# Feed forward of a decoder layer: outputs split by tiles of tokens, gate units in threes, two banks for the last down projections

## The chip, the cores and the metric

The kernel is one program on one core of a Trainium2 chip. The number is the device time of an execution in microseconds. In the profile PE is TensorE, DVE VectorE, ACT ScalarE, POOL GpSimd and SP the engine that only issues transfers.

## What is computed

A decoder layer in float32, with a layer norm behind each part. Cut to what matters:

```python
x = layernorm(x + self_attention(x))                     # x: 32 x 100 x 512, 3200 tokens
x = layernorm(x + cross_attention(x, ctx_1024))          # 16 heads of 32, context 32 x 722 x 512
gate = x @ (w_gate / 127).T                              # w_gate, w_up: 1536 x 512 integers
up = x @ (w_up / 127).T
x = layernorm(x + (silu(gate) * up) @ (w_down / 127).T)  # w_down: 512 x 1536
```

The change touches what happens from the output projection of the cross attention on.

## The kernel before

The program runs in stages: self attention; cross attention; and a last one, which this document calls the feed forward. It takes the 3200 tokens in `NG` = 5 groups of `GT` = 640, a group in `TT` = 5 tiles of 128 tokens or in two halves of 320. To keep float32 accuracy, an activation is split into a high part (rounded to the format of the fast products, written by ScalarE) and a low part (what is left, by VectorE or GpSimd), and TensorE sums the products of both.

The order of each engine's instructions is written out by hand; semaphores hold the engines together, and the names of the semaphores say what has been done. For a group `g` the work is:

- `gate_and_up(g)` on TensorE: `HU` = 24 units, one for each chunk of 128 hidden features and each half of the group; 8 products of 320 columns into `ps_g` and 8 into `ps_u`, with two banks each. `silu_and_high` (ScalarE), `gate` (VectorE) and `low_h` (GpSimd) turn a unit into the high and low half of the hidden activations `hs`. The function `unit(u)` says which chunk and half the unit `u` is.
- `down(g, i)` for each tile `i` on TensorE: 24 products of 512 columns into the single bank `ps_d`. VectorE takes it with `third_sum` (adds `x2`, then statistics), GpSimd computes the factor (`rstd_of`), and VectorE norms with `third_norm`; the tile is stored.
- between those, for the group ahead, `project_o(g+1, i)`: 12 products of 512 columns from the split outputs of the cross attention, `acts`, into the single bank `ps_y`; `second_sum` and `normalise("a", ...)` on VectorE make the tile `x2`; `transpose_x2(g+1, i-1)` transposes it with four products into `ps_t`, and `high_x2` (ScalarE) and `low_x2` (VectorE) split it into `acts` again, now the input of the next gate units.

The body of the loop on TensorE shows this order:

```python
gate_and_up(g)
for i in range(TT):
    down(g, i)
    project_o(g + 1, i)
    if i:
        transpose_x2(g + 1, i - 1)
```

The last tile's transpose, `transpose_x2(g, TT - 1)`, stands behind the first gate unit of its group. `acts` can be overwritten with the next group's outputs only when the last gate unit has read them; then `high_o` (ScalarE) and `low_o` (VectorE) split the raw tile `oraw`, before in `KD` = 4 chunks of 128 features by 640 tokens. On VectorE `low_o(g+1)` stands ahead of `third_sum(g, 0)`. Group 0 and the last group are written apart; in group 0 the weights are still arriving and ScalarE converts them between the units (`CONVERT_AT`), and the last two `weighted_sum` of the cross attention are done there (`RESULT_AT`). In the last group only the five `down` are left behind the units.

## Time and profile before

| what | us |
|---|---|
| median of 3 runs | 2518.63 |
| lowest and highest | 2517.06, 2522.48 |
| the profiled execution | 2520.11 |
| its span, first to last instruction | 2518.3 |
| TensorE busy in the span | 2437.4 |

The span is what the trace covers; the profiled execution's own time is 1.8 us longer. A row of the order of time gives an instruction's start, its duration, its engine and line, what it writes and reads, and in brackets how long the engine stood idle before it and who released it.

### The profile page before, as it was taken

How to read it: one execution, taken by the hardware profiler on the slowest of the kernel's cores; microseconds unless marked ns; L12 is line 12 of the kernel's file. 1: busy time of each engine (PE TensorE's matmuls, PEld its weight loads, DVE VectorE, ACT ScalarE, POOL GpSimd, SP SyncE). 2: the span in 40 equal slices, each digit the busy share in tenths (PEclk: the TensorE clock that was granted, in tenths of full speed). 3: DMA queues.
4: the chain of work that ended last, by engine and by line, in shares of the span. 5: the costliest groups of instructions: out<-in, count | busy, mean ns of one | idle time of the engine just before them, and what ended most of it. 6: DMA issues, size and time to landing. Idle time of an engine off the chain costs nothing.

```text
span 2518.3 us, 58619 instructions
## 1 busy us (share of the span) xinstructions
PE 2437.4 (97%) x22240; PEld 2089.1 (83%) x22240; DVE 1532.8 (61%) x2589; ACT 1253.1 (50%) x2451; POOL 1323.4 (53%) x1058
## 2 busy tenths in 40 slices
PE   7999998988999999999999999999999899999998
PEld 7888866887888888888888888888888698998997
DVE  7555567863666666666667666666666725335342
ACT  3544453104666666666666666666666651221311
POOL 4766554314656666665666666565665532333332
PEclk9999988998999999999999999999999999999999
DMA  7554455633777766777777777777777841101010
GB/s 226 164 149 140 131 155 200 243 125 106 191 189 193 189 186 183 188 189 187 194 190 189 185 183 190 188 187 193 189 188 191 233 137 63 39 25 63 0 38 22
DMA packets 259625, 391.61 MB, mean 156 GB/s; under 512 B 123164, under 2 KB 140572, under 8 KB 259356
## 3 DMA queue, kind: packets, MB, share of 16 engines
q1 hardware_dynamic: 234780, 337.66, 46.8%
q10 hardware_dynamic: 24576, 50.36, 8.3%
q8 instruction: 169, 2.77, 0.5%
q14 instruction: 100, 0.82, 0.1%
HBM read 134.11 MB, written 52.43 MB: 74 GB/s over the span
## 4 chain that ended last, share of the span: by engine, by line
PE 63%; issue 8%; DVE 2%; DMA 1%; SPq 1%; POOL 1%; ACT 1%; POOLq 0%; ACTq 0%; DVEq 0%
PE D_ps_p L68 41%; PE D_ps_s L1719 7%; PE D_ps_p L1745 6%; PE E_ps_g L68 3%; PE E_ps_u L68 3%; PE E_ps_d L68 2%; PE E_ps_y L68 1%; SPq L1171 1%; DMA D_pT<-D_turned 1%; POOL E_hidden_low L1322 0%; DVE D_neg_max L1529 0%; DMA E_w_int<-in_w_gate 0%; POOL E_rstd_a L1309 0%; DVE D_turned L1543 0%; ACT D_e L1394 0%
## 5 line engine op out<-in xcount | busy, mean ns | idle before, releaser
L1278 POOL TENSOR_SCALAR D_e<-D_e,D_inv 128x722 f32<-128x722 f32 x256 | 538.9, 2105 | 539.3 <-DVE D_inv L1535 539.3
L1394 ACT ACTIVATE D_e<-D_ps_s,D_neg_max 128x723 f32<-128x723 f32 x512 | 438.2, 862 | 409.4 <-DVE D_neg_max L1529 358.7
L1529 DVE TENSOR_REDUCE D_neg_max<-D_ps_s 128x1 f32<-128x723 f32 x512 | 439.5, 899 | 313.4 <-PE D_ps_s L1719 313.4
L1543 DVE STREAM_TRANSPOSE D_turned<-D_e 128x768 f32<-128x768 f32 x512 | 496.2, 972 | 6.6 <-DMA D_pT<-D_turned 6.1
L68 PE MATMUL D_ps_p<-D_ctx_high,cross_wk_high 128*128 128x362 f32 (+1 forms) x1024 | 351.1, 343 | 12.4 <-DVE D_ctx_low L1560 12.3
L68 PE MATMUL D_ps_p<-D_ctx_low,cross_wk_high 128*128 128x362 f32 (+1 forms) x1024 | 337.4, 329 | 0.0
L68 PE MATMUL D_ps_p<-D_ctx_high,cross_wk_low 128*128 128x362 f32 (+1 forms) x1024 | 335.9, 328 | 0.0
L68 PE MATMUL D_ps_p<-cross_wv_high,D_ctx_high 128*128 128x512 f32 (+1 forms) x768 | 303.8, 396 | 0.0
L68 PE MATMUL D_ps_p<-cross_wv_high,D_ctx_low 128*128 128x512 f32 (+1 forms) x768 | 303.3, 395 | 0.0
L68 PE MATMUL D_ps_p<-cross_wv_low,D_ctx_high 128*128 128x512 f32 (+1 forms) x768 | 301.7, 393 | 0.0
L1401 ACT ACTIVATE D_e<-D_e,D_inv 128x722 f32<-128x722 f32 x256 | 231.0, 902 | 8.0 <-DVE D_inv L1535 8.0
L68 PEld LDWEIGHTS D_ps_p<-D_ctx_high,cross_wk_high 128*128 128x128 f32 x1024 | 193.3, 189 | 35.1 <-issue 32.1
L1293 POOL TENSOR_TENSOR D_ctx_low<-D_craw,D_ctx_high 128x722 fp32r<-128x722 f32 x124 | 198.9, 1604 | 17.4 <-issue 6.8
L1322 POOL TENSOR_TENSOR E_hidden_low<-E_gated,E_hidden_high 128x320 fp32r<-128x320 f32 x120 | 105.2, 878 | 189.0 <-ACT E_hidden_high L1459 189.0
L68 PEld LDWEIGHTS D_ps_p<-D_ctx_low,cross_wk_high 128*128 128x128 f32 x1024 | 194.1, 190 | 2.7
L1719 PE MATMUL D_ps_s<-D_keys,D_queries 32*128 32x241 f32 (+1 forms) x3072 | 193.5, 380 | 2.7 <-ACT D_e L1394 2.7
L68 PEld LDWEIGHTS D_ps_p<-D_ctx_high,cross_wk_low 128*128 128x128 f32 x1024 | 193.9, 189 | 0.0
L1639 DVE SCALAR_TENSOR_TENSOR E_gated<-E_ps_u,E_gated 128x320 f32<-128x320 f32 x120 | 58.9, 491 | 215.5 <-ACT E_gated L1466 215.5
L1719 PEld LDWEIGHTS D_ps_s<-D_keys,D_queries 32*128 32x128 f32 x3072 | 135.1, 185 | 60.9 <-issue 50.6
L68 PEld LDWEIGHTS D_ps_p<-cross_wv_high,D_ctx_low 128*128 128x128 f32 (+1 forms) x768 | 139.1, 181 | 39.6
L1389 ACT ACTIVATE D_values<-D_ps_p 128x512 f32<-128x512 f32 x192 | 114.4, 596 | 106.4 <-PE D_ps_p L68 105.9
L68 PEld LDWEIGHTS D_ps_p<-cross_wv_low,D_ctx_high 128*128 128x128 f32 (+1 forms) x768 | 139.7, 182 | 29.7
(189 smaller groups left out, 5087.5 us busy)
## 6 DMA issues: line engine op xcount, KB each, us to landing
D_pT<-D_turned SPq DMA_DIRECT2D x1536, 96.0 KB, 2.8
D_pT<-D_turned ACTq DMA_DIRECT2D x512, 96.0 KB, 2.9
D_craw<-in_ctxT SPq DMA_DIRECT2D x126, 361.0 KB, 3.8
self_q<-A_q_out SPq DMA_DIRECT2D x10, 640.0 KB, 3.8
self_k<-A_k_out SPq DMA_DIRECT2D x10, 640.0 KB, 3.2
self_v<-A_v_out SPq DMA_DIRECT2D x25, 256.0 KB, 2.1
A_q<-self_q SPq DMA_DIRECT2D x32, 200.0 KB, 3.9
A_k<-self_k SPq DMA_DIRECT2D x32, 200.0 KB, 4.3
```

Source lines behind the costliest of these rows:

```text
L68: last = pe.matmul(out, lhs(a, k), rhs(b, k), start=(k == 0 and n == 0), stop=(k == chunks - 1 and n == len(terms) - 1))
L1278: pool.tensor_scalar(head, head, inv[:, 2 * (s % 2):2 * (s % 2) + 1], None, ALU.mult)\
L1293: pool.tensor_tensor(cs[b % 2][1][:, k, :], craw[k % 2][:, :], cs[b % 2][0][:, k, :].bitcast(F32), ALU.subtract).then_inc(c_low, 1)
L1322: pool.tensor_tensor(hs[1][:, c, cols], gated[u % 2][:, :], hs[0][:, c, cols].bitcast(F32), ALU.subtract).then_inc(hl_done, 1)
L1389: act.activation(vs[b % 2][0:rows, i, :], bank("v", b, i)[0:rows, 0:D], ACT.Copy).then_inc(v_done, 1)
L1394: act.activation(e[n // 2 % 2][:, n % 2, 0:PARTS * PART].rearrange("p (a c) -> p a c", a=PARTS), parts_of(n), ACT.Exp, bias=neg_max[:, n % ...
L1401: act.activation(head, head, ACT.Copy, scale=inv[:, 2 * (s % 2) + 1:2 * (s % 2) + 2])\
L1529: dve.tensor_reduce(neg_max[:, n % 4:n % 4 + 1], parts_of(n), AX.XY, ALU.max, negate=True)\
L1543: dve.transpose(turned[quad % 2][:, :, 2 * (s % 2) + h, :].rearrange("p j (t r) -> p t j r", r=32), e[s % 2][:, h, :].rearrange("p (t j r) ...
L1639: dve.scalar_tensor_tensor(gated[u % 2][:, :], ps_u[u % 2][:, 0:HALF], FSCALE, gated[u % 2][:, :], ALU.mult, ALU.mult).then_inc(h_done, 1)
L1719: return pe.matmul(of_head[:, j, a, 0:end - first], qs[rows, m, :, :].rearrange("p a q -> p (a q)"), ks[rows, m, first:end], start=True, s ...
L1745: last = pe.matmul(out[HD * j:HD * (j + 1), 0:T], vs[b % 2][:, i, c:c + HD], pT[quad % 2][:, :, j, 32 * i:32 * i + QB], start=(i == 0), st ...
```

## The change

Four things change. The outputs of the cross attention are split in five operations of 4 x 128 elements, one for each tile of tokens, instead of four of 640, and each `project_o` waits only for its own tile. The gate units go in threes: three chunks for the first half of the group, then the same three for the second half (before in pairs); the first unit that reads the second half is now `u == 3`. The last tile is transposed, and its high and low halves made, behind the second unit instead of the first. In the last group the down projections use `ps_d` and `ps_y` in turn, and wait for the sum of the tile two before.

```diff
--- before.py
+++ after.py
@@ -1111,7 +1111,7 @@
 
 
 
-            return 2 * (u // 4) + u % 2, u // 2 % 2
+            return 3 * (u // 6) + u % 3, u // 3 % 2
 
         def groups(eng, body):
 
@@ -1129,6 +1129,10 @@
                 return (w_gate, w_up)[n % 2].rearrange("(k p) n -> p k n", p=P)[:, :, n // 2 * FC:(n // 2 + 1) * FC]
             k = (n - 2 * KD) * (KF // KD)
             return w_down[k * P:(k + KF // KD) * P, :].rearrange("(a p) n -> p a n", p=P)
+
+        def split_before(g):
+
+            return KD + TT * (g - 1) if isinstance(g, int) else g * TT + (KD - TT)
 
         def x1_rows(g, i):
 
@@ -1175,7 +1179,7 @@
 
                 def load_o(g):
                     if later(g):
-                        sp.wait_ge(o_low, KD * g)
+                        sp.wait_ge(o_low, split_before(g))
                     sp.dma_start(oraw[:, :, :], eo_rows[:, :, col(g * GT, GT)]).then_inc(o_loaded, 16)
 
                 def load_x1(g, i):
@@ -1437,8 +1441,9 @@
                     act.wait_ge(o_loaded, 16 * g + 16)
                     if later(g):
                         act.wait_ge(gu_done, HU * g)
-                    for k in range(KD):
-                        act.activation(acts[0][:, k, :], oraw[:, k, :], ACT.Copy).then_inc(o_high, 1)
+                    for i in range(TT):
+                        cols = slice(i * P, (i + 1) * P)
+                        act.activation(acts[0][:, :, cols], oraw[:, :, cols], ACT.Copy).then_inc(o_high, 1)
 
                 def high_x2(g, i):
                     act.wait_ge(t_done, TT * g + i + 1)
@@ -1465,10 +1470,10 @@
                         wait(act, hl_done, n - 1)
                         act.activation(gated[u % 2][:, :], ps_g[u % 2][:, 0:HALF], ACT.Silu, scale=FSCALE)\
                            .then_inc(silu_done, 1)
-                        if u == 0:
+                        if u > 0:
+                            high(u - 1)
+                        if u == 1:
                             high_x2(g, TT - 1)
-                        else:
-                            high(u - 1)
                         if not later(g):
                             for piece_n in CONVERT_AT.get(u, ()):
                                 convert(piece_n)
@@ -1605,21 +1610,22 @@
                     dve.wait_ge(x1b_done, n + 1)
                     add_and_stats("a", n, lambda dst: dve.tensor_tensor(dst, ps_y[:, :], x1_rows(g, i), ALU.add))
 
-                def third_sum(g, i):
+                def third_sum(g, i, down=ps_d):
                     n = TT * g + i
                     dve.wait_ge(d_done, n + 1)
                     add_and_stats("b", n, lambda dst: dve.scalar_tensor_tensor(
-                        dst, ps_d[:, :], FSCALE, x2[:, i, :], ALU.mult, ALU.add))
+                        dst, down[:, :], FSCALE, x2[:, i, :], ALU.mult, ALU.add))
 
                 def third_norm(g, i):
                     wait(dve, out_stored[i % 2], 16 * slot_count(g, i))
                     normalise("b", TT * g + i, y[i % 2][:, :])
 
                 def low_o(g):
-                    for k in range(KD):
-                        dve.wait_ge(o_high, KD * g + k + 1)
+                    for i in range(TT):
+                        cols = slice(i * P, (i + 1) * P)
+                        dve.wait_ge(o_high, split_before(g) + i + 1)
                         dve.wait_ge(o_loaded, 16 * g + 16)
-                        dve.tensor_tensor(acts[1][:, k, :], oraw[:, k, :], acts[0][:, k, :].bitcast(F32),
+                        dve.tensor_tensor(acts[1][:, :, cols], oraw[:, :, cols], acts[0][:, :, cols].bitcast(F32),
                                           ALU.subtract).then_inc(o_low, 1)
 
                 def low_x2(g, i):
@@ -1638,7 +1644,7 @@
                         dve.wait_ge(silu_done, n + 1)
                         dve.scalar_tensor_tensor(gated[u % 2][:, :], ps_u[u % 2][:, 0:HALF], FSCALE, gated[u % 2][:, :],
                                                  ALU.mult, ALU.mult).then_inc(h_done, 1)
-                        if u == 0:
+                        if u == 1:
                             low_x2(g, TT - 1)
                         if not later(g) and u in RESULT_AT:
                             take_result(RESULT_AT[u])
@@ -1686,7 +1692,7 @@
                 groups(dve, body)
                 gate(NG - 1)
                 for i in range(TT):
-                    third_sum(NG - 1, i)
+                    third_sum(NG - 1, i, (ps_d, ps_y)[i % 2])
                     third_norm(NG - 1, i)
 
             @block.tensor
@@ -1752,9 +1758,10 @@
 
                 def project_o(g, i):
                     n = TT * g + i
-                    if i == 0:
-                        pe.wait_ge(o_low, KD * (g + 1))
-                    if not later(n):
+                    if later(g):
+                        pe.wait_ge(o_low, split_before(g) + i + 1)
+                    elif i == 0:
+                        pe.wait_ge(o_low, KD)
                         pe.wait_ge(wo_low, KD)
                         pe.wait_ge(k_done, KU * B)
                         pe.wait_ge(v_done, ST * B)
@@ -1784,7 +1791,7 @@
                                 pe.wait_ge(int_done, 2 * (c // 3 + 1))
                             if u == 0:
                                 pe.wait_ge(tl_done, TT * g + (HALF + P - 1) // P)
-                            if u == 2:
+                            if u == 3:
                                 pe.wait_ge(tl_done, TT * (g + 1))
                             wait(pe, h_done, n - 1)
                             for ps, which in ((ps_g, 0), (ps_u, 1)):
@@ -1792,22 +1799,24 @@
                                                 lambda a, k: place(w, 2 * (c // 3) + which)[:, k, c % 3 * P:(c % 3 + 1) * P],
                                                 lambda a, k: view(acts[a][:, k, h * HALF:(h + 1) * HALF]))
                             last.then_inc(gu_done, 1)
-                            if u == 0:
+                            if u == 1:
                                 transpose_x2(g, TT - 1)
                             if not later(g) and u in RESULT_AT:
                                 weighted_sum(RESULT_AT[u])
 
-                    def down(g, i):
+                    def down(g, i, out=ps_d):
                         n = TT * g + i
                         if not later(g) and i == 0:
                             pe.wait_ge(int_done, PIECES)
                             pe.wait_ge(o_done, QUADS * B)
                         if i == 0:
-                            pe.wait_ge(hl_done, HU * (g + 1) - 2)
+                            pe.wait_ge(hl_done, HU * (g + 1) - 3)
                         if i == 2:
                             pe.wait_ge(hl_done, HU * (g + 1))
-                        wait(pe, sum_done["b"], n)
-                        products(pe, ps_d[:, :], ((0, 0), (1, 0)), KF,
+                        if out is ps_y:
+                            pe.wait_ge(sum_done["a"], TT * NG)
+                        wait(pe, sum_done["b"], n - (1 if isinstance(g, int) and g == NG - 1 and i else 0))
+                        products(pe, out[:, :], ((0, 0), (1, 0)), KF,
                                  lambda a, k: view(hs[a][:, k, i * P:(i + 1) * P]),
                                  lambda a, k: w[2 * KD + k // 3][:, k % 3 * D:(k % 3 + 1) * D]).then_inc(d_done, 1)
 
@@ -1830,7 +1839,7 @@
                     groups(pe, body)
                     gate_and_up(NG - 1)
                     for i in range(TT):
-                        down(NG - 1, i)
+                        down(NG - 1, i, (ps_d, ps_y)[i % 2])
 
                 for s in range(FIRST, MAIN + 1):
                     if 0 <= s < STEPS and s % 2 == 0:
```

ScalarE at the start of a group in the loop: the silu and the hidden copy of units 0 and 1 (`E_gated`, `E_hidden_high`), and the last tile's high half from `E_ps_t0`. Before:

```order
L1466 ACTIVATE E_gated0_8136<-E_ps_g0 128x320 [waits E_hl_done]
L1444 ISA
L1445 ACTIVATE E_acts_high_8112<-E_ps_t0 128x4x128 [waits E_t_done]
L1464 REGISTER_ALU
L1466 ACTIVATE E_gated1_8137<-E_ps_g1 128x320 [waits E_hl_done,E_gu_done]
L1459 ACTIVATE E_hidden_high_8138<-E_gated0_8136 128x320 [waits E_h_done]
L1464 REGISTER_ALU
L1466 ACTIVATE E_gated0_8136<-E_ps_g0 128x320 [waits E_hl_done,E_gu_done]
```

and now:

```order
L1471 ACTIVATE E_gated0_8136<-E_ps_g0 128x320 [waits E_hl_done]
L1469 REGISTER_ALU
L1471 ACTIVATE E_gated1_8137<-E_ps_g1 128x320 [waits E_hl_done,E_gu_done]
L1464 ACTIVATE E_hidden_high_8138<-E_gated0_8136 128x320 [waits E_h_done]
L1449 ISA
L1450 ACTIVATE E_acts_high_8112<-E_ps_t0 128x4x128 [waits E_t_done]
L1469 REGISTER_ALU
L1471 ACTIVATE E_gated0_8136<-E_ps_g0 128x320 [waits E_hl_done,E_gu_done]
L1464 ACTIVATE E_hidden_high_8138<-E_gated1_8137 128x320 [waits E_h_done]
```

The high half of the last tile has moved from behind the first silu to behind the second silu and the first hidden copy.

VectorE at the boundary behind group 0: `low_o(1)` from `E_oraw`, then the sum and the statistics of the first down projection (`E_ps_d`). Before:

```order
L1639 SCALAR_TENSOR_TENSOR E_gated_8137<-E_ps_u,E_gated_8137 128x320 [waits E_silu_done,E_gu_done]
L1622 TENSOR_TENSOR E_acts_low<-E_oraw,E_acts_high 128x640 [waits E_o_loaded,E_o_high] x4
L1611 SCALAR_TENSOR_TENSOR E_r_b<-E_ps_d,E_x_8134 128x512 [waits E_d_done]
L1590 BN_STATS E_stats_b<-E_r_b 128x6 [waits E_sum_b]
L1592 BN_AGGR E_mv_b<-E_stats_b 128x2 [waits E_stat_b]
L1594 TENSOR_SCALAR E_var_eps_b<-E_mv_b 128x1 [waits E_mv_b]
```

and now:

```order
L1645 SCALAR_TENSOR_TENSOR E_gated_8137<-E_ps_u,E_gated_8137 128x320 [waits E_silu_done,E_gu_done]
L1628 TENSOR_TENSOR E_acts_low<-E_oraw,E_acts_high 128x4x128 [waits E_o_loaded,E_o_high] x5
L1616 SCALAR_TENSOR_TENSOR E_r_b<-E_ps_d,E_x_8134 128x512 [waits E_d_done]
L1595 BN_STATS E_stats_b<-E_r_b 128x6 [waits E_sum_b]
L1597 BN_AGGR E_mv_b<-E_stats_b 128x2 [waits E_stat_b]
L1599 TENSOR_SCALAR E_var_eps_b<-E_mv_b 128x1 [waits E_mv_b]
```

Four operations on 640 elements have become five on 4 x 128, all of them still ahead of the sum.

TensorE in the last group, from the end of the first down projection to the start of the second (the weights are `E_w_f32r8` to `11`). Before:

```order
L68 MATMUL E_ps_d<-E_w_f32r11_8175,E_hidden_low_8139 128x512
L68 MATMUL E_ps_d<-E_w_f32r11_8175,E_hidden_high_8138 128x512
L68 MATMUL E_ps_d<-E_w_f32r11_8175,E_hidden_low_8139 128x512
L68 MATMUL E_ps_d<-E_w_f32r8_8172,E_hidden_high_8138 128x512 [waits E_sum_b]
L68 MATMUL E_ps_d<-E_w_f32r8_8172,E_hidden_low_8139 128x512
L68 MATMUL E_ps_d<-E_w_f32r8_8172,E_hidden_high_8138 128x512
```

and now:

```order
L68 MATMUL E_ps_d<-E_w_f32r11_8175,E_hidden_low_8139 128x512
L68 MATMUL E_ps_d<-E_w_f32r11_8175,E_hidden_high_8138 128x512
L68 MATMUL E_ps_d<-E_w_f32r11_8175,E_hidden_low_8139 128x512
L68 MATMUL E_ps_y<-E_w_f32r8_8172,E_hidden_high_8138 128x512 [waits E_sum_b,E_sum_a]
L68 MATMUL E_ps_y<-E_w_f32r8_8172,E_hidden_low_8139 128x512
L68 MATMUL E_ps_y<-E_w_f32r8_8172,E_hidden_high_8138 128x512
```

The second projection writes to another bank and waits for sums that lie further back.

## Rows read from the trace of the kernel before

**Rows 1.** The page, busy time, share of the span and instructions.
```profile
PE 2437.4 (97%) x22240; PEld 2089.1 (83%) x22240; DVE 1532.8 (61%) x2589; ACT 1253.1 (50%) x2451; POOL 1323.4 (53%) x1058
```

**Rows 2.** The waits of TensorE from 2005 us on: total, times, longest.
```profile
PE E_ps_y L68 <- DVE E_acts_low L1622: 4.8, 4, 1.2
...
PE E_ps_d L68 <- DVE E_r_b L1611: 3.2, 4, 0.9
PE E_ps_t L1771 <- DVE E_x L1599: 2.5, 5, 0.7
PE E_ps_g L68 <- DVE E_gated L1639: 1.7, 1, 1.7
```

**Rows 3.** TensorE in order of time at a group's boundary: start, duration.
```profile
2180.89 0.39 PE L68 MATMUL E_ps_d<-E_w_f32r,E_hidden_low 128*128 128x512 f32 x1
...
2182.49 0.50 PE L68 MATMUL E_ps_y<-E_wo_high,E_acts_high 128*128 128x512 f32 x1 [1.21 <-DVE E_acts_low L1622]
...
2185.13 0.39 PE L68 MATMUL E_ps_y<-E_wo_high,E_acts_low 128*128 128x512 f32 x1
2185.36 0.39 PE L68 MATMUL E_ps_d<-E_w_f32r,E_hidden_high 128*128 128x512 f32 x1
...
2190.57 0.39 PE L68 MATMUL E_ps_d<-E_w_f32r,E_hidden_low 128*128 128x512 f32 x1
...
2193.29 0.40 PE L68 MATMUL E_ps_y<-E_wo_high,E_acts_low 128*128 128x512 f32 x1
...
2193.89 0.48 PE L68 MATMUL E_ps_d<-E_w_f32r,E_hidden_high 128*128 128x512 f32 x1
```

**Rows 4.** The other engines at that boundary; last, the subtractions' minimum, median, maximum (ns).
```profile
2178.14 4.29 DVE L1622 TENSOR_TENSOR E_acts_low<-E_oraw,E_acts_high 128x640 fp32r<-128x640 f32 x4 [1.26 <-ACT E_acts_high L1441]
2182.35 0.68 DVE L1611 SCALAR_TENSOR_TENSOR E_r_b<-E_ps_d,E_x 128x512 f32<-128x512 f32 x1
2177.29 2.61 ACT L1441 ACTIVATE E_acts_high<-E_oraw 128x640 fp32r<-128x640 f32 x4
2178.40 1.88 POOL L1304 TENSOR_TENSOR E_x1b<-E_x1b,E_bo_b 128x512 f32<-128x512 f32 x1
L1622 DVE TENSOR_TENSOR E_acts_low<-E_oraw,E_acts_high x4: 810/894/1917, 2178.1 to 2181.6; 128x640 fp32r<-128x640 f32 x4
```

**Rows 5.** A group's start: TensorE, ScalarE, VectorE; L1459 by line.
```profile
2222.12 0.31 PE L68 MATMUL E_ps_u<-E_acts_low,E_w_f32r 128*128 128x320 f32 x1
2222.90 0.66 PE L1771 MATMUL E_ps_t<-ident,E_x 128*128 128x128 f32 x4 [0.47 <-DVE E_x L1599]
2223.31 0.39 PE L68 MATMUL E_ps_g<-E_acts_high,E_w_f32r 128*128 128x320 f32 x1
...
2225.74 0.31 PE L68 MATMUL E_ps_g<-E_acts_high,E_w_f32r 128*128 128x320 f32 x1
2222.55 0.44 ACT L1466 ACTIVATE E_gated<-E_ps_g 128x320 f32<-128x320 f32 x1 [1.82 <-PE E_ps_u L68]
2223.59 0.60 ACT L1445 ACTIVATE E_acts_high<-E_ps_t 128x512 fp32r<-128x512 f32 x1 [0.61 <-PE E_ps_t L1771]
L1459 ACT ACTIVATE E_hidden_high<-E_gated 128x320 fp32r<-128x320 f32 x120 | 55.6, 463 | 1.4 <-DVE E_gated L1639 1.4
2224.29 0.69 DVE L1629 TENSOR_TENSOR E_acts_low<-E_ps_t,E_acts_high 128x512 fp32r<-128x512 f32 x1 [0.45 <-ACT E_acts_high L1445]
```

**Rows 6.** Group 0 in order of time: TensorE's transposes, ScalarE's third conversion.
```profile
2014.56 0.66 PE L1771 MATMUL E_ps_t<-ident,E_x 128*128 128x128 f32 x4 [0.39 <-DVE E_x L1599]
2025.11 1.49 ACT L1497 ACTIVATE E_w_f32r<-E_w_int 128x1536 fp32r<-128x1536 int32 x1 [2.98 <-DMA E_w_int<-in_w_gate]
```

**Rows 7.** First and last product of the last group's five down projections.
```profile
2480.80 0.39 PE L68 MATMUL E_ps_d<-E_w_f32r,E_hidden_high 128*128 128x512 f32 x1
2512.23 0.39 PE L68 MATMUL E_ps_d<-E_w_f32r,E_hidden_low 128*128 128x512 f32 x1
```

**Rows 8.** The last 38 us: busy times by engine, then the granted clock (0.98).
```profile
2480.00:2518.30 38.30, 29.39 (x127) 22.82 (x125) 11.83 (x26) 1.27 (x3) 4.87 (x8) 0.98 0.10 36
```

## The prediction

> **What bounds the kernel now.** I read the page first, then the waits of the last stage, then that stage in order of time. The page has TensorE busy for 97% of the span [rows 1]; the other engines reach at most 61%. The change touches the feed forward alone, the last 507 us, so its worth is read there: whatever it takes from another engine is worth nothing unless TensorE stood still for it. The list of waits from 2005 us on names the idle times of TensorE [rows 2]: 4.8 us in four waits of `project_o`, the cross attention's output projection, for the low halves of its activations; 3.2 us in four waits of a down projection for the sum that empties its bank; 2.5 us in five waits of the transposes for the normalised tile; 1.7 us once for a gated product. The change aims at all but the last. An idle time is less than what a stall costs, since the first product after it starts slowly, so I take each cost as a difference between first and last starts in order of time.
>
> **The change, part by part.** Four parts; each is costed on TensorE.
>
> *The split of the cross attention's outputs by tiles of tokens.* Before, `project_o(g+1, 0)` waits until all four chunks are split. From the start of the last product of the down projection before it to the start of its own last product 4.24 us pass (2180.89 to 2185.13); where nothing is missing it is 2.72 us (2190.57 to 2193.29) [rows 3]. The stall costs 1.52 us, and there are four such places [rows 2]: 6.1 us. Afterwards tile 0 needs one ScalarE and one VectorE operation. ScalarE starts the copies at 2177.29 and VectorE the first subtraction at 2178.14; four take 4.29 us, one of them 1.92 us and the shortest 0.81 [rows 4]. Even if the long one comes first, tile 0 is split by 2178.1 + 1.9 = 2180.0, and TensorE asks for it at 2180.89 + 0.23 = 2181.12. So the whole 1.52 us goes. What is late next is `third_sum(g, 0)`: it stands behind all of `low_o` on VectorE, and `down(g, 1)` waits for it, since both use `ps_d`. It began at 2182.35 and took 0.68 [rows 4]; with as many elements in five operations instead of four I put it at the same place plus 0.1, done by 2183.15. TensorE will want the bank at 2181.12 + 2.72 = 2183.84. The cover is 0.7 us, and before it was 2.3 us (2185.36). Nothing else on VectorE or GpSimd is pushed: the second sum and both norms follow the earlier projection.
>
> The price of an operation on 4 x 128 elements from the raw tile is not in the trace. From below it is the 0.69 us of the subtraction of 4 x 128 from PSUM [rows 5], from above the 1.92 us of the slowest subtraction of 640 [rows 4]. I take 0.7 for those undisturbed and one delay of 1.1 us as before (1.92 less 0.81), which gives 0.7 x 5 + 1.1 = 4.6, less small overlaps. The long row lies beside GpSimd's addition at 2178.40, which took 1.88 us [rows 4]; only GpSimd's last subtraction and that one addition are queued there, so five small operations meet the same two instructions.
>
> The Trainium skill says (VectorE: DVE Perf Modes, on the TRN2 errata) that each instruction from SBUF pays a fixed cost, and gives (N+151)/0.96 ns for such a subtraction. The trace agrees at 640: 824 ns against the fastest, 810. By it five of 512 cost 0.16 us more than four of 640, which would speak against the split but stays inside its cover. It also says (SBUF — State Buffer, Who interferes with whom) that a VectorE operation with two SBUF inputs and a GpSimd operation that reads SBUF shut each other out for a whole instruction; the 1.92 and 1.88 us side by side agree, and by that rule there is again one delay, not five.
>
> *The last tile's transposes, behind the second gate unit instead of the first.* Before, TensorE ended the first unit at 2222.12 (start of its last product) and could transpose only at 2222.90, and the next unit began at 2223.31: 1.19 us [rows 5]. Where the tile is there, last product to first product across a transpose is 0.60 us (2193.29 to 2193.89) [rows 3]. The loss is 0.59 for an idle time of 0.47, thus 0.12 above it. The five waits hold 2.5 us, 0.39 of them in group 0 [rows 2, 6]; the other four cost 2.1 + 4 x 0.12 = 2.6 us. The tile's norm ends about when it did, and one more unit (2.43 us, 2223.31 to 2225.74) lies ahead of the transpose, so this wait goes entirely.
>
> It is replaced by a tighter one. The low half of the tile must be there at the fourth unit (`u == 3`) instead of the third. Counted from the start of the second unit's last product: ScalarE starts the silu 0.43 later (2222.12 to 2222.55) and needs 0.44, then the copy of the hidden half, 0.46, then the tile's high half, 0.60; VectorE starts 0.70 after that last one starts and needs 0.69 [rows 5]. That is 0.43 + 0.44 + 0.46 + 0.70 + 0.69 = 2.72. TensorE comes to the fourth unit at 0.60 + 2.43 = 3.03. There are 0.3 us left, where before 2225.74 less 2224.98 left 0.8. I cost it at nothing.
>
> *Units in threes.* 24 units a group of the same 16 products each; only the order of chunk and half changes. `down(g, 0)` now waits for 21 of 24 low halves instead of 22, all of the first half of the group, so it asks for less. Nothing.
>
> In group 0 there is a wait that stays. ScalarE's third conversion there stood still for 2.98 us for a transfer of weights and began at 2025.11 [rows 6]; the silu behind it was late, and TensorE stood still for 1.7 us [rows 2]. That transfer hangs on nothing in the change, and the conversion keeps its place at `u == 2`. Whatever TensorE gains before (the 0.39 us) it waits longer here. I count nothing in group 0 up to the end of that wait.
>
> *Two banks in the last group.* The five down projections run from 2480.80 to 2512.23 (first start to last start), 31.43 us [rows 7]. Unhindered, one is 5.21 us from first to last start (2185.36 to 2190.57) and 0.23 to the next [rows 3]: 4 x 5.44 + 5.21 = 26.97. That saves 4.5 us. Each sum and norm ends well within the 5.44 us of the next projection, and with `sum_done` asked for two tiles back no wait is left. What follows 2512.23, 6.1 us to the end of the span, stays.
>
> **Sum.** 6.1 + 2.6 + 4.5 = 13.2 us. The profiled execution took 2520.1 us (span 2518.3 and 1.8 around it), so it would become 2506.9. It lies 1.5 us above the median of the runs, 2518.63, and against that the sum gives 2505.5 us, my forecast. TensorE's granted clock reads 0.98 in the stretch with the pauses of the last five projections, close to the full 2.4 GHz [rows 8], so fewer pauses change no product's rate by more than that.
>
> **Rivals.**
> 1. *The boundary's gain is given back one projection later*: `third_sum(g, 0)` is late and `down(g, 1)` waits. For it speaks that the cover is just 0.7 us and that `low_o` was once held up by 1.1 us. Against it, that one hold-up is already in my time. If it took two delays more, 0.7 us would be covered and 1.5 of 2.2 lost at each of four places: all 6.1 us, and the time is 2511.6. Chance 12%.
> 2. *The fourth unit waits for the last tile's low half.* ScalarE's queue is the reason: one more copy ahead of it, 0.3 us of cover. If each link takes 0.25 us more than in the rows, 0.7 us are lost in four groups, 2.8 us: 2508.3. Chance 8%.
> 3. *The change does little at the starts and ends of groups*: both stalls are formed anew in full, and only the two banks count: 2514.1. It needs 1 and 2 together at full size. Chance 5%.
> 4. *Slower.* The strided operations of `low_o` all cost the upper bound: 2178.1 + 5 x 1.92 = 2187.7, the sum ends at 2188.4, and `down(g, 1)` starts 3.0 us later than the 2185.36 of before, which is 12.0 us in four groups against 2.6 + 4.5 gained elsewhere: 2523.5. It decides from 1.75 us a group, so when the five take 8.4 us or 1.7 each. For it there is the one of four at that price [rows 4], against it that the GpSimd work beside them ends after two instructions. Chance 3%.
> 5. *More than the sum*: the transfer in group 0 lands early enough, or the first tiles gain too; at most 0.4 + 1.7 more, 2503.4. Chance 4%.
>
> **Numbers.** My forecast has 68%. The three runs lie from 1.6 us below their median to 3.9 above; its own range is 2503 to 2508.5. Rivals 1 and 2 reach to 2511.6, rival 5 with a fast run to 2501.9. From 2501.5 to 2512 about 2 in 10 or less is left out (rivals 3 and 4, and the spread of the runs). A change under 0.2% (5.0 us) can't be told from none: rival 3 and a part of 4 and of 1 fall there, 8%; slower 3%; faster 89%.
>
> **What would show it.** In the profile after: no wait of `E_ps_y` for `E_acts_low` and none of `E_ps_d` for `E_r_b` in the last group; no wait of the transposes for `E_x` except in group 0; groups 2.1 us closer together; five down projections in 27.0 us. A new wait of `E_ps_d` for `E_r_b` behind the first projection of a group shows rival 1 and, from 3 us on, rival 4; one of `E_ps_g` for `E_acts_low` shows rival 2. The prediction is wrong if the five subtractions take over 5.3 us together.

## The result

The changed kernel takes 2507.75 us (median of 5 runs, 2503.35 to 2510.46) against 2518.63 before; the ratio is 0.9949, with 0.9933 to 0.9964 as its interval. Measured again, beside two of the kernels below, it was 0.9959 (0.9946 to 0.9973), 2507.80 us. The forecast was 2505.5, range 2501.5 to 2512. The profiled execution took 2508.33 us, its span 2506.5: 11.8 us less than the span of before, where the sum had 13.2.

The page's busy line, to compare with [rows 1]: TensorE does the same products in 11.8 us less span, and its share is still 97%.

```profile
PE 2432.2 (97%) x22240; PEld 2089.1 (83%) x22240; DVE 1535.0 (61%) x2593; ACT 1251.4 (50%) x2455; POOL 1319.6 (53%) x1058
```

The waits of TensorE from 2005 us on, in the changed kernel (total, times, longest), to compare with [rows 2]:

```profile
PE E_ps_y L68 <- DVE E_r_a L1611: 3.2, 1, 3.2
PE E_ps_g L68 <- DVE E_gated L1645: 2.7, 1, 2.7
PE E_ps_g L68 <- DVE E_acts_low L1635: 1.1, 1, 1.1
```

The four waits of `project_o` for the low halves, the four of the last down projections for the sum and all five of the transposes are gone. The wait of 3.2 us is the one that was there before, ahead of group 0. The wait for a gated product has grown from 1.7 to 2.7 us.

**A group's boundary.** TensorE in order of time: the last product of the first down projection, the first and last of `project_o`, and the next down projection.

```profile
2180.16 0.39 PE L68 MATMUL E_ps_d<-E_w_f32r,E_hidden_low 128*128 128x512 f32 x1
...
2180.38 0.39 PE L68 MATMUL E_ps_y<-E_wo_high,E_acts_high 128*128 128x512 f32 x1
...
2182.88 0.39 PE L68 MATMUL E_ps_y<-E_wo_high,E_acts_low 128*128 128x512 f32 x1
2183.10 0.39 PE L68 MATMUL E_ps_d<-E_w_f32r,E_hidden_high 128*128 128x512 f32 x1
...
2188.32 0.39 PE L68 MATMUL E_ps_d<-E_w_f32r,E_hidden_low 128*128 128x512 f32 x1
```

From 2180.16 to 2182.88 are 2.72 us, where [rows 3] had 4.24. VectorE beside it, and the five subtractions by tile (minimum, median, maximum in ns):

```profile
2177.31 4.46 DVE L1628 TENSOR_TENSOR E_acts_low<-E_oraw,E_acts_high 128x512 fp32r<-128x512 f32 x5 [1.16 <-ACT E_acts_high L1446]
2181.69 0.68 DVE L1616 SCALAR_TENSOR_TENSOR E_r_b<-E_ps_d,E_x 128x512 f32<-128x512 f32 x1
```

```profile
L1628 DVE TENSOR_TENSOR E_acts_low<-E_oraw,E_acts_high x5: 678/679/1780, 2177.3 to 2181.1; 128x512 fp32r<-128x512 f32 x5
```

Five operations on 4 x 128 elements take 4.46 us, four of 640 took 4.29 [rows 4]. Three of the five take 0.68 us; the first takes 0.95, and the second again takes long, 1.78, beside GpSimd's addition. Before, it was the same two: 0.98 and 1.92 us, the others 0.81. The sum ends at 2182.37 and TensorE asks for the bank at 2183.10: a cover (time to spare before TensorE would have to wait) of 0.7 us, as forecast.

**A group's start.** TensorE with the last tile's transposes, now behind the second unit, and VectorE's low half of that tile:

```profile
2222.21 0.31 PE L68 MATMUL E_ps_u<-E_acts_low,E_w_f32r 128*128 128x320 f32 x1
2222.36 0.60 PE L1778 MATMUL E_ps_t<-ident,E_x 128*128 128x128 f32 x4
2222.72 0.39 PE L68 MATMUL E_ps_g<-E_acts_high,E_w_f32r 128*128 128x320 f32 x1
...
2225.15 0.31 PE L68 MATMUL E_ps_g<-E_acts_high,E_w_f32r 128*128 128x320 f32 x1
2223.95 0.69 DVE L1635 TENSOR_TENSOR E_acts_low<-E_ps_t,E_acts_high 128x512 fp32r<-128x512 f32 x1 [0.36 <-ACT E_acts_high L1450]
```

From the last product before the transposes to the first behind them are 0.51 us, against 1.19 in [rows 5]. The low half is done at 2224.64; the unit that needs it starts at 2225.15. So 0.5 us are left; I had forecast 0.3.

**The last group.** First product of the first, first product of the second (into the other bank), and last product of the fifth down projection:

```profile
2473.44 0.39 PE L68 MATMUL E_ps_d<-E_w_f32r,E_hidden_high 128*128 128x512 f32 x1
...
2478.90 0.39 PE L68 MATMUL E_ps_y<-E_w_f32r,E_hidden_high 128*128 128x512 f32 x1
...
2500.44 0.39 PE L68 MATMUL E_ps_d<-E_w_f32r,E_hidden_low 128*128 128x512 f32 x1
```

These are 27.00 us from first to last, where [rows 7] had 31.43; 26.97 was forecast.

**Group 0.** TensorE before and behind its pause, and ScalarE's third conversion:

```profile
2024.87 0.31 PE L68 MATMUL E_ps_u<-E_acts_low,E_w_f32r 128*128 128x320 f32 x1
2027.89 0.39 PE L68 MATMUL E_ps_g<-E_acts_high,E_w_f32r 128*128 128x320 f32 x1 [2.70 <-DVE E_gated L1645]
...
2028.40 0.31 PE L68 MATMUL E_ps_g<-E_acts_low,E_w_f32r 128*128 128x320 f32 x1
...
2029.50 0.47 PE L68 MATMUL E_ps_u<-E_acts_high,E_w_f32r 128*128 128x320 f32 x1
...
2031.77 1.37 PE L1751 MATMUL D_ps_p<-D_pT,D_values 128*32 128x100 f32 x48
2025.34 1.48 ACT L1502 ACTIVATE E_w_f32r<-E_w_int 128x1536 fp32r<-128x1536 int32 x1 [4.01 <-DMA E_w_int<-in_w_gate]
```

The conversion behind the transfer of weights starts almost when it did (2025.34 against 2025.11 in [rows 6]), but TensorE comes earlier and stands still for 2.70 us, 1.03 more than before. Counted from the first gate product of group 0 (2011.40, before 2011.58), TensorE begins its last product ahead of the pause at 13.47 us, before at 14.10: that is 0.6 of the 1.03 us. The conversion begins at 13.94, before at 13.53: the other 0.4 is a later transfer. Then something new: the products of 320 columns, 0.31 us long at 2028.40, are 0.47 us long at 2029.50. The stages show why (the number behind the busy times is the granted clock):

```profile
2024.00:2028.00 4.00, 1.30 (x10) 1.06 (x9) 0.49 (x1) 2.17 (x3) 0.42 (x1) 1.00 0.04 15
2028.00:2030.00 2.00, 2.00 (x10) 2.00 (x11) 0.49 (x1) 0.79 (x2) 1.04 (x2) 0.67 0.00 0
2030.00:2032.00 2.00, 2.00 (x15) 1.67 (x18) 0.00 (x0) 0.13 (x1) 0.27 (x1) 0.50 0.00 0
2032.00:2034.00 2.00, 2.00 (x54) 1.85 (x47) 0.77 (x2) 0.67 (x2) 0.87 (x1) 0.98 0.04 12
```

The clock reads 0.50, the lower level of 1.2 GHz, from 2030 to 2032; in all it is low for 3.4 us, which this document calls a slow stretch. Before, behind the pause of 1.67 us, it was full:

```profile
2026.00:2028.00 2.00, 0.34 (x2) 0.37 (x3) 0.49 (x1) 1.27 (x3) 0.65 (x1) 1.00 0.00 0
2028.00:2030.00 2.00, 2.00 (x16) 1.98 (x14) 0.49 (x1) 0.80 (x2) 1.03 (x2) 1.00 0.00 0
```

From the pause's end to the weighted sum (2027.89 to 2031.77) pass 3.88 us; before it was 2.51 for the same work (2027.66 to 2030.17). The slow stretch alone costs 1.4 us.

### The profile page after: what moved, and what is told of

It reads as the page before. It is cut to its first block, busy times and chain, and to the rows that moved or that the text cites. A ratio compares the mean times of both kernels' runs of the same rounds, so it can differ in the third digit from the quotient of the medians.

```text
span 2506.5 us, 58637 instructions
## 1 busy us (share of the span) xinstructions
PE 2432.2 (97%) x22240; PEld 2089.1 (83%) x22240; DVE 1535.0 (61%) x2593; ACT 1251.4 (50%) x2455; POOL 1319.6 (53%) x1058
## 4 chain that ended last, share of the span: by engine, by line
PE 72%; DVE 1%; issue 1%; DMA 1%; SPq 1%; ACT 1%; POOL 0%; ACTq 0%; DVEq 0%; POOLq 0%
PE D_ps_p L68 41%; PE D_ps_s L1725 7%; PE D_ps_p L1751 6%; PE E_ps_u L68 5%; PE E_ps_g L68 5%; PE E_ps_d L68 5%; PE E_ps_y L68 3%; SPq L1175 1%; ACT D_e L1398 0%; DVE D_neg_max L1534 0%; PE E_ps_t L1778 0%; DMA D_pT<-D_turned 0%; DMA E_w_int<-in_w_gate 0%; DVE D_turned L1548 0%; DMA D_values<-in_ctxT 0%
```

## The experiments

Each ratio is to the kernel before as measured on the same chip. The runs of one kernel lie 3 to 12 us apart, and what lies ahead of the first gate product makes much of that: in the twelve profiled executions of this study it starts between 2009.40 and 2014.19 us. Two times of a few us apart are therefore read in three pieces of one trace each, from a start to a start of TensorE's products, which leave that out: group 0 (first gate product to first down projection), the groups between (to the first down projection of the last group) and the last five projections (to their last product).

| kernel | ratio to before (interval) | group 0 | between | last five | pause in group 0 |
|---|---|---|---|---|---|
| before | | 62.12 | 407.10 | 31.43 | 1.67 |
| changed | 0.9949 (0.9933 to 0.9964) | 64.01 | 398.03 | 27.00 | 2.70 |
| changed, again | 0.9959 (0.9946 to 0.9973) | 62.08 | 398.03 | 27.00 | 2.26 |
| split alone | 0.9966 (0.9953 to 0.9979) | 60.87 | 400.96 | 31.45 | 0.42 |
| threes and late transposes alone | 0.9985 (0.9976 to 0.9994) | 64.52 | 404.11 | 31.44 | 3.18 |
| two banks alone | 0.9987 (0.9977 to 0.9997) | 62.18 | 406.99 | 26.99 | 1.72 |
| changed, late conversion | 0.9933 (0.9921 to 0.9946) | 59.58 | 398.03 | 26.99 | none |
| the same, again | 0.9933 (0.9919 to 0.9946) | 59.58 | 398.02 | 27.00 | none |
| before, late conversion | 0.9989 (0.9980 to 0.9998) | 60.23 | 406.94 | 31.48 | none |
| late transposes in pairs | 1.0036 (1.0022 to 1.0050) | 62.23 | 413.79 | 31.44 | 1.60 |
| subtractions twice | 1.0006 (0.9996 to 1.0016) | 62.76 | 409.91 | 27.00 | 2.91 |
| before, early conversion | 1.0018 (1.0008 to 1.0028) | 66.85 | 407.00 | 31.44 | 4.86 |

The pieces "between" and "last five" repeat within 0.2 us where the kernels do the same there. Group 0 does not, for the transfer of weights comes at another time in each execution: the third conversion begins 13.53 us behind the first gate product before, 13.58 with two banks alone, 12.27 with the split alone, 14.42 with the threes and late transposes alone, 13.94 and 13.49 in the two traces of the changed kernel, 14.17 with the subtractions twice. TensorE's last product ahead of the pause begins at 14.09 or 14.10 in the kernels whose order of units and transposes is the old one and at 13.47 to 13.50 where it is the new one. In all nine traces with a pause, those of the early conversion (14.37 and 11.75) and of the late transposes in pairs (13.63 and 14.28) included, the pause is the first of these numbers less the second plus 2.24 us, to 0.01. So 0.6 us of a pause come from the change, and the rest of its differences from the transfer.

**The split alone.** The kernel before with `high_o`, `low_o`, `split_before` and the waits of `project_o` and of the load from the changed one:

```diff
-                    for k in range(KD):
-                        act.activation(acts[0][:, k, :], oraw[:, k, :], ACT.Copy).then_inc(o_high, 1)
+                    for i in range(TT):
+                        cols = slice(i * P, (i + 1) * P)
+                        act.activation(acts[0][:, :, cols], oraw[:, :, cols], ACT.Copy).then_inc(o_high, 1)
```

> The kernel before with only the split of the cross attention's outputs by tiles. Theory of additive stalls: the four waits of TensorE for E_acts_low vanish, 4 x 1.52 = 6.1 us less, 2512.5 us; the wait in group 0 stays near 1.7 us and the clock full there, since nothing ahead of it is earlier. Rival (given back one projection later): a wait of the second down projection for E_r_b at each of four boundaries, and a time above 2515.

Measured: 2513.41 us, 8.0 below the 2521.46 of before on that chip. The groups between are 6.14 us shorter, as the theory had it, and no wait of a down projection for `E_r_b` came up between them. That group 0 keeps its pause of 1.7 us did not come true: it was 1.25 us shorter in this execution and its pause 0.42 us, since the transfer came 1.26 us earlier (12.27 against 13.53). The part does not touch it.

**The units in threes and the late transposes alone.** `unit`, the places of `transpose_x2`, `high_x2` and `low_x2` and the two counts:

```diff
-            return 2 * (u // 4) + u % 2, u // 2 % 2
+            return 3 * (u // 6) + u % 3, u // 3 % 2
...
-                            if u == 0:
+                            if u == 1:
                                 transpose_x2(g, TT - 1)
```

> The kernel before with only the units in threes and the last tile's transposes behind the second unit. Theory that group 0 gives a part back because of this part: four group starts gain 3.0 us, TensorE comes earlier to the wait for the converted weights in group 0, stands still for over 2 us instead of 1.7, and then runs for some 4 us at the lower clock, 1.4 to 1.7 us lost; 2517 us. Rival (the longer pause and the lower clock were chance in that run and have nothing to do with the change): 3.0 us gained whole, 2515.6 us, clock full behind the pause.

Measured: 2517.46 us. Between the groups 2.99 us less. In group 0 the pause is 3.18 us, and behind it the way to the weighted sum takes 3.43 us instead of 2.51 at the slow clock:

```profile
2029.39 0.39 PE L68 MATMUL E_ps_g<-E_acts_high,E_w_f32r 128*128 128x320 f32 x1 [3.18 <-DVE E_gated L1639]
...
2032.82 1.50 PE L1745 MATMUL D_ps_p<-D_pT,D_values 128*32 128x100 f32 x30
2026.84 1.48 ACT L1497 ACTIVATE E_w_f32r<-E_w_int 128x1536 fp32r<-128x1536 int32 x1 [4.49 <-DMA E_w_int<-in_w_gate]
```

So group 0 is 2.4 us longer and the part is worth 0.6 us net in this trace. That is what the theory had, but not all of it is due to the part: of the 1.51 us by which the pause is longer, 0.9 come from a late transfer (the last row, 14.42 us behind the first gate product at 2012.42, against 13.53) and 0.6 from TensorE's earlier arrival.

**The two banks alone.** `down` and `third_sum` with the bank as an argument, `ps_d` and `ps_y` in turn in the last group:

```diff
-                        down(NG - 1, i)
+                        down(NG - 1, i, (ps_d, ps_y)[i % 2])
```

> The kernel before with only the two banks in the last group. Additive stalls: the five down projections take 27.0 us instead of 31.4, 2514.2 us, and nothing else moves; pause in group 0 near 1.7 us with the clock full. Rival that the granted clock falls at the end without pauses: five projections above 28 us.

The five projections take 26.99 us, 4.4 less, and nothing else moves. The median, 2518.70 us against 2521.46 before on that chip, gives 2.8 us; the interval of the ratio (0.8 to 5.8 us) does not tell that from 4.4.

The gains of the three parts between the groups and at the end, 6.14 + 2.99 + 0.11 = 9.24 and 4.4, add up to those of the changed kernel, 9.07 and 4.4, within 0.2. No part takes from another there by more than that.

**The conversion moved away from the transfer.** The changed kernel, and one word of a table:

```diff
-    CONVERT_AT = {0: (2,), 1: (3,), 2: (4,), 9: (5,), 11: (6,), 13: (7,), 15: (8,), 17: (9,), 19: (10,), 21: (11,)}
+    CONVERT_AT = {0: (2,), 1: (3,), 7: (4,), 9: (5,), 11: (6,), 13: (7,), 15: (8,), 17: (9,), 19: (10,), 21: (11,)}
```

> The changed kernel with ScalarE's conversion of weight piece 4 behind unit 7 of group 0 instead of unit 2; the piece is needed from unit 12. If the wait of ScalarE for that transfer is the whole cause of the pause in group 0, the pause (2.7 us) and the slow clock behind it (1.5 us) both go: 4.3 us less than the changed kernel, 2503.4 us. Rival (the lower clock comes from something else, such as the pause of 3.2 us ahead of group 0): only the pause goes, 2505 us, and the clock still reads half for some us near the same place.

> The changed kernel with the late conversion, beside the changed kernel on one chip. Theory of group 0: 4.3 us below it, ratio to before 0.9932, no wait for E_gated, full clock from the first gate unit on. Rival (the time moves elsewhere): under 2 us below it.

Measured: 2504.63 and, again, 2501.94 us, the fastest kernel of the study. In group 0 there is no pause and no slow stretch. TensorE in the second run of it, from the first gate product of group 0 to the last weighted sum:

```profile
2009.45 0.39 PE L68 MATMUL E_ps_g<-E_acts_high,E_w_f32r 128*128 128x320 f32 x1 [1.14 <-DVE E_acts_low L1635]
...
2025.50 0.73 PE L1751 MATMUL D_ps_p<-D_pT,D_values 128*32 128x100 f32 x24
```

That is 16.05 us against 20.37 in the changed kernel's first trace (2011.40 to 2031.77), 4.3 less. Beside the changed kernel on one chip:

> The changed kernel once more, on the same chip as the late conversion. 13.5 us from the four parts less 1.7 us in group 0: ratio 0.995 to 0.996. Theory of group 0: a pause of TensorE for E_gated of 2.5 to 3.2 us and a stretch at the lower clock behind it. Rival (chance in the first run): pause below 2 us and full clock.

Measured 2507.80 us. This time the pause was 2.26 us, between the theory's 2.5 to 3.2 and the rival's 2, and the clock stayed full, as the rival had it:

```profile
2028.85 0.38 PE L68 MATMUL E_ps_g<-E_acts_high,E_w_f32r 128*128 128x320 f32 x1 [2.26 <-DVE E_gated L1645]
...
2031.37 1.25 PE L1751 MATMUL D_ps_p<-D_pT,D_values 128*32 128x100 f32 x48
```

```profile
2025.00:2029.00 4.00, 1.74 (x12) 1.51 (x12) 0.49 (x1) 2.17 (x3) 0.46 (x1) 1.00 0.03 11
2029.00:2031.00 2.00, 2.00 (x15) 2.00 (x16) 0.49 (x1) 0.80 (x2) 1.03 (x2) 1.00 0.00 0
```

Group 0 took 62.08 us, no more than before. So the loss of 1.9 us in the first trace isn't a fixed price of the change. The late conversion's group 0 is 2.5 us shorter than this one and 4.4 us shorter than the first; the medians are 5.9 us apart with no overlap of the runs (2500.80 to 2503.91, 2507.33 to 2510.99). That is more than the 4.3 expected: in these two traces the first gate product itself starts 3.36 us apart (2009.45 and 2012.81), which the late conversion, coming after it, can't have caused.

**The same word in the kernel before.**

> The kernel before with the late conversion alone. It has only the short pause of 1.7 us and no slow stretch behind it, so theory: 1.8 to 2.0 us less than before, ratio 0.9993, against 4.3 us in the changed kernel. Rival (the slow stretch does not hang on the pause's length): as much as in the changed kernel, 4 us or more.

Measured: 2516.82 us, ratio 0.9989 (0.9980 to 0.9998), and group 0 1.9 us shorter: the pause and its restart, no slow stretch. That is the theory's number. It is the trace that speaks against the rival's 4 us; the interval of the ratio (0.5 to 5.0 us) would allow it.

**Late transposes, units in pairs.** The kernel before with only the three places of the last tile moved, so that the third unit needs what the second has just let pass:

> The kernel before with the last tile's transposes behind the second unit but the units still in pairs, so the third unit needs the tile at once. The chain from the prediction ends 2.72 us after the second unit's last product starts, and TensorE comes there at 0.60: a wait of E_ps_g for E_acts_low of 1.9 to 2.1 us in each of five groups, in place of the 0.6 us lost now; 4 x 1.5 = 6 us slower in the later groups, 2525 us, and group 0 about as before. A measured wait longer than 2.4 us would mean that the threes only just cover the chain; rival 2 of the prediction needs one over 2.7.

Measured: 2529.53 us, slower than before. TensorE at the third unit of group 2:

```profile
2230.85 0.41 PE L68 MATMUL E_ps_g<-E_acts_high,E_w_f32r 128*128 128x320 f32 x1 [1.80 <-DVE E_acts_low L1629]
```

The wait is 1.80 us in three groups, 1.73 in the last (1.9 to 2.1 were expected) and 0.77 in group 0, and the groups between take 6.7 us more. A unit takes 2.43, so the threes cover this chain with about half a microsecond to spare, as the trace of the changed kernel shows directly. Without the threes, moving the transposes costs 6.7 us instead of gaining 3.0. Of the 6.7, 1.3 us a group are the longer wait, and 1.5 are a slow stretch of 3.4 us that came behind the wait of 1.80 us in group 3 alone:

```profile
2333.93 0.41 PE L68 MATMUL E_ps_g<-E_acts_high,E_w_f32r 128*128 128x320 f32 x1 [1.80 <-DVE E_acts_low L1629]
...
2335.76 0.47 PE L68 MATMUL E_ps_u<-E_acts_low,E_w_f32r 128*128 128x320 f32 x1
```

**Each subtraction twice.** In `low_o` of the changed kernel, in place of the single subtraction; the counts in `load_o` and `project_o` follow:

```diff
+                        for again in range(2):
+                            if again:
+                                dve.wait_ge(o_low, low_before(g) + 2 * i + 1)
+                            dve.tensor_tensor(acts[1][:, :, cols], oraw[:, :, cols], acts[0][:, :, cols].bitcast(F32),
+                                              ALU.subtract).then_inc(o_low, 1)
```

> The changed kernel with each of the five subtractions of the outputs done twice, the second waiting for the first, from the same operands into the same place. In the changed kernel's trace the sum behind them ends 0.7 us before TensorE asks for its bank. Theory (cover of 0.7 us, then one for one): the five take 4 to 4.5 us longer, the second down projection waits 3.3 to 3.8 us for E_r_b at four boundaries, 14 to 16 us above the changed kernel, so slower than before by 2 to 4 us. If TensorE's wait is under 2 us, the price of rival 4 in the prediction was too high.

Measured: 2520.98 us, on a chip where before took 2521.21. At a boundary (TensorE: last product of the first down projection, last of `project_o`, first of the next down projection; VectorE: the ten subtractions, the sum):

```profile
2181.42 0.39 PE L68 MATMUL E_ps_d<-E_w_f32r,E_hidden_low 128*128 128x512 f32 x1
...
2184.14 0.39 PE L68 MATMUL E_ps_y<-E_wo_high,E_acts_low 128*128 128x512 f32 x1
2187.20 0.50 PE L68 MATMUL E_ps_d<-E_w_f32r,E_hidden_high 128*128 128x512 f32 x1 [2.67 <-DVE E_r_b L1620]
2178.57 7.97 DVE L1635 TENSOR_TENSOR E_acts_low<-E_oraw,E_acts_high 128x512 fp32r<-128x512 f32 x10 [1.16 <-ACT E_acts_high L1450]
2186.46 0.68 DVE L1620 SCALAR_TENSOR_TENSOR E_r_b<-E_ps_d,E_x 128x512 f32<-128x512 f32 x1
```

The ten take 7.97 us, 3.51 more than the five. TensorE waits 2.67 us, 2.97 are lost a group, 11.9 in four. 3.51 less 2.97 is 0.5: near the cover of 0.7 us read from the trace, less the slow restart. So rival 4's mechanism exists, and in the one size tried what lies beyond the cover is lost in full. I had expected waits of 3.3 to 3.8 us and 14 to 16 us in all, since I took the repeated operations at 0.8 to 0.9 us where an undisturbed one takes 0.68.

**The conversion one unit earlier.** The kernel before with `1: (3, 4)` in the table.

> The kernel before with the conversion of piece 4 behind unit 1 instead of unit 2, so ScalarE stands still for the same transfer one unit earlier and TensorE stops one unit earlier too, while the transfer lands at the same time. Theory (a pause of some 4 us lets the clock fall, one of 1.7 does not): pause of 3.5 to 4.5 us for E_gated, a stretch of some us at the lower clock behind it, and 2.4 + 1.5 = 3.9 us more than before in group 0. Rival (the lower clock in the changed kernel comes from the units in threes or the earlier start): full clock behind the pause and 2.4 us more.

Measured: 2524.61 us, ratio 1.0018. The pause is 4.86 us, and the way from its end to the weighted sum (one unit more than before, 2.35 us) takes 6.39 us instead of 4.86; the clock is low behind it:

```profile
2026.45 0.47 PE L68 MATMUL E_ps_g<-E_acts_high,E_w_f32r 128*128 128x320 f32 x1 [4.86 <-DVE E_gated L1639]
...
2032.84 0.38 PE L1745 MATMUL D_ps_p<-D_pT,D_values 128*32 128x100 f32 x8
```

```profile
2026.00:2028.00 2.00, 1.55 (x6) 1.58 (x7) 0.67 (x2) 0.86 (x3) 0.90 (x2) 0.65 0.00 0
2028.00:2030.00 2.00, 2.00 (x9) 2.00 (x9) 0.12 (x1) 0.00 (x0) 0.83 (x1) 0.50 0.00 0
2030.00:2032.00 2.00, 2.00 (x15) 2.00 (x14) 0.49 (x1) 0.80 (x2) 0.52 (x1) 1.00 0.00 0
```

Group 0 is 4.7 us longer, 3.2 by the pause and 1.5 by the clock. So neither the threes nor the earlier start is needed for the slow stretch; a longer pause alone came with it in the kernel before. But the run with doubled subtractions, whose group 0 is that of the changed kernel, stood still for 2.91 us and kept its clock:

```profile
2027.66 0.39 PE L68 MATMUL E_ps_g<-E_acts_high,E_w_f32r 128*128 128x320 f32 x1 [2.91 <-DVE E_gated L1652]
...
2030.17 1.25 PE L1758 MATMUL D_ps_p<-D_pT,D_values 128*32 128x100 f32 x48
```

```profile
2024.50:2027.50 3.00, 0.24 (x2) 0.00 (x0) 0.48 (x1) 2.17 (x3) 0.15 (x1) 1.00 0.00 2
2027.50:2029.50 2.00, 1.84 (x13) 1.87 (x14) 0.50 (x2) 0.80 (x2) 1.03 (x2) 1.00 0.00 0
```

I had said that the length of the pause decides. It does not alone: in group 0 the clock stayed full behind 0.4, 1.7, 2.3 and 2.91 us and fell behind 2.70, 3.18 and 4.86. In the same run of doubled subtractions it stayed full behind all four waits of 2.67 us, and with the late transposes in pairs it fell behind one of three waits of 1.80 and not behind the one of 1.73. That theory falls in this form: a pause of 1.8 to 2.9 us can cost the slow stretch or not.

There is one more slow stretch, in every trace and untouched by any of these edits. Ahead of group 0 TensorE waits 3.2 us for a tile's sum on VectorE, and the clock falls around its restart. In the kernel before, products of 512 columns then take 0.63 us instead of 0.39:

```profile
2005.12 0.79 PE L68 MATMUL E_ps_y<-E_wo_high,E_acts_high 128*128 128x512 f32 x1 [3.23 <-DVE E_r_a L1606]
2006.14 0.63 PE L68 MATMUL E_ps_y<-E_wo_high,E_acts_low 128*128 128x512 f32 x1
```

It lasts 3.4 us in ten of the twelve traces and 6.8 in two, the changed kernel's second and the split alone, whose way from that restart to the first gate product is about 1.2 us longer. This is a part of what moves the start of group 0.

## Why the prediction was right

*The split by tiles*: 6.1 us forecast, 6.1 measured (alone, between the groups). The unknown price, 0.7 us for an undisturbed operation with one delay of 1.1 us, was 0.68 and 1.10; a second, small delay of 0.27 us of the first operation, 0.16 before, was not in my sum of 4.6 us and was made up by the overlaps (4.46). The cover of `third_sum` was 0.7 us as worked out. Rival 1 did not come: it needed two long delays beyond the one in the sum, and none came.

*The late transposes*: 2.6 us forecast, 3.0 measured. The mechanism was right and the term was mis-sized, short by 0.09 us a group, because I took the undisturbed passage over a transpose from a place behind products of 512 columns (0.60 us); behind products of 320 columns it takes 0.51. The new wait at the fourth unit has 0.5 us of cover instead of the 0.3 I gave it. The chain took 2.43 us (2222.21 to 2224.64) instead of 2.72, 0.2 of it because ScalarE starts one operation before the one ahead of it has ended and I had added whole durations. Rival 2 did not come, and with neither 1 nor 2 there was nothing of rival 3.

*Units in threes, no cost*: none shows, and they are what makes the second part possible (late transposes in pairs: 6.7 us slower). Threes without the late transposes were not run.

*Two banks*: 4.5 us forecast, 4.4 measured.

*Group 0, nothing*: the one step that failed in the first trace. That the gain ahead of the pause is swallowed by it was right, though it is 0.6 us and not 0.39: in the second trace of the changed kernel group 0 takes 62.08 us against 62.12. But I wrote that fewer pauses change no product's rate, and did not ask what one longer pause does: in the first trace, and with the threes alone, the clock fell behind it and group 0 took 1.9 and 2.4 us more. I also took the transfer's time as fixed, where it moved by 2.1 us against the first gate product from trace to trace. Rival 5, that it lands early enough, is what happened by chance in the split alone; in the changed kernel's first trace it landed later. The transfer is where the next 2.5 to 4.4 us lay, and one number in a table takes them.

The sum, 13.2 us, stands against 13.5 in the feed forward of the second trace (500.65 less 487.11) and 11.6 in that of the first. The medians gave 10.9 us, then 12.0, within what the time ahead of group 0 varies by. That the first median lies within 2.3 us of the forecast is therefore in part luck; what the traces bear out is the mechanism and size of the three gains.

## What to carry to other kernels

Where one engine is busy for 97% of the span, list its waits one by one and cost each from last start to last start, not by its idle time: the first product behind a wait starts slowly, and here a stall of 1.2 us cost 1.5. Read the reference for an undisturbed passage from products of the same size. Before a wait is moved, work out the chain that must fit into its new cover (here three operations on two other engines against one unit of 2.43 us), and look for the waits on transfers behind it: an engine that comes earlier to a transfer only waits longer, and may pay for it twice.

## What the runs showed of the hardware

Behind some pauses of TensorE its granted clock read 0.50, 1.2 GHz instead of 2.4, for 3.4 us, and products of 320 columns took 0.47 us instead of 0.31. In the changed kernel it fell about 0.8 us after TensorE had resumed, with the threes and late transposes alone 1.3 us after; behind the longest pause it was low almost from the start (0.47 us at 2026.45). It also fell around the end of the wait of 3.2 us ahead of group 0, in all twelve traces, for 6.8 us in two of them. In group 0 the fall followed pauses of 2.70, 3.18 and 4.86 us and did not follow one of 2.91 us or any up to 2.26. In the later groups it followed one wait of 1.80 us and did not follow two others of 1.80 or four of 2.67. So the length of the pause does not decide alone, and what does I can't say from these runs.

The Trainium skill (SBUF — State Buffer, Who interferes with whom) has a VectorE operation with two SBUF inputs and a GpSimd one that reads SBUF contend for a shared port that one of them holds alone. The traces agree that the two hold each other up: one of four operations of 640 took 1.92 us instead of 0.81, and one of five of 512 took 1.78 instead of 0.68, the same 1.1 us whether the work is cut in four or five, and GpSimd's addition beside it took 1.88 and 1.75 us where its median is 1.30 and 1.29.
